# A decoder layer's feed-forward stage: Relu, squares and low part over two hidden units at a time

## The chip, the cores and the metric

The kernel runs on one core of a Trainium2 chip. The metric is the device time of one execution in microseconds (us), lower is better. The core has five engines that work in parallel, each from its own queue in order: PE (TensorE, matmuls), DVE (VectorE), ACT (ScalarE), POOL (GpSimd) and SP (SyncE, which issues DMAs here). They wait for each other through semaphores.

## The reference

A decoder layer over 8 batches of 512 tokens with 256 features: linear attention, cross-attention with 16 heads, and a feed-forward part, each followed by a layer norm. Only the feed-forward part matters here:

```python
def _bitlinear(x, w_latent):
    scale = jnp.clip(jnp.mean(jnp.abs(w_latent), axis=1, keepdims=True), 1e-05, None)
    tern = jnp.clip(jnp.round(w_latent / scale), -1.0, 1.0)
    return x @ (tern * scale).T          # in effect

h = _bitlinear(x, w_fc) + gate * (x @ v.T @ fast_b.T @ u.T)    # 256 -> 1024
r = jnp.maximum(h, 0.0)
y = _bitlinear(r * r, w_proj)                                  # 1024 -> 256
x = _layernorm(x + y)
```

## The kernel before

Activations lie with the features on the 128 partitions and a batch's 512 tokens along the columns. The three parts of the layer run one after the other; `ffn_phase` is the last. A batch is two tiles of 512 columns (features 0 to 127 and 128 to 255). The hidden layer of 1024 is eight tiles of 128 x 512, called units here, i = 0 to 7.

Full precision comes from splitting: a value is rounded to the type fp32r ("hi") and the rest is kept as a second fp32r tile ("lo"), and a product is summed from hi x hi, hi x lo and lo x hi. So a unit's hidden matmul is six PE instructions (`split_matmul`, L47 to L49). For each unit then
- ACT takes Relu from the unit's PSUM bank into the tile relu (`r`, L1280), and squares it with rounding into `h_hi` (L1284);
- POOL squares `r` in full precision into the tile relu2 (`rr`, L1242);
- DVE subtracts `h_hi` from `rr` and writes the low part `h_lo` (L1373, `hidden_lo`);
- PE projects with the ternary weights, `h_hi` and `h_lo` in turn (L1484, L1485).

`r` and `rr` hold four units in a ring (RH = 4). The units' PSUM banks are 0, 1, 2 and 7; bank 3 holds the statistics of the third norm (STAT3), bank 4 those of the second (STAT2), banks 5 and 6 the projection's output.

Two layer norms are woven between the units, written out by hand in each engine's queue. While batch b is in its units, the second norm of batch b+1 is made (names with a 2: mean by PE at L1455, `deviate2` on DVE, square on ACT at L1254, `sum_squares2` on DVE, variance by PE at L1459, root on ACT, `normalise2` on DVE, which ends with x_hi and x_lo, L1365 and L1367), and the third norm of batch b-1 (names with a 3: `residual` and `sum_y3` on DVE, mean at L1465, `deviate3`, `sum_squares3`, variance at L1469, `normalise3`, then the store). PE begins batch b+1 when x_lo of b+1 is there. DVE's queue in a batch is: residual, sum_y3, low parts 0 and 1, deviate2, low part 2, sum_squares2, low part 3, deviate3, low parts 4 and 5, sum_squares3, low parts 6 and 7, normalise2, the sum for the mean of b+2, normalise3. In the views a tile's name drops its number: `y_sum<-y` is sum_y3, `y_sum<-y_c` that of the second norm, `dev<-y,ps` is deviate3, `cx_lo` is x_lo, and both `r` and `rr` read "relu".

## Time and profile before

| what | us |
|---|---|
| median of 3 runs (lowest, highest) | 1464.99 (1464.03, 1467.11) |
| the profiled execution's own time | 1464.29 |
| its span, from first to last instruction | 1462.5 |
| granted clock of PE, mean over the span | 0.976 of full |

| engine | busy us | share |
|---|---|---|
| PE | 1364.8 | 93% |
| DVE | 961.9 | 66% |
| ACT | 807.1 | 55% |
| POOL | 618.5 | 42% |

The feed-forward stage is the last seventh of the span, from about 1235 us on; the rest belongs to the two attentions. A share over the whole span is a mean over stages with different limits. The views used are the table of stretches (busy time by engine in a window), the chain of waits (followed back from the last instruction to whatever released each step), the timeline of an engine, and the instruction groups. In a timeline, a row with x2 merges two instructions; what stands in brackets is the engine's idle time before it and who ended it. PE's matmuls overlap, so its busy time is not its time at peak.

### The profile page before, as it was taken

Reading aid. Unit: us, or ns where it says so; the run is one execution under the profiler, and the core shown is the slowest. Engines: PE = TensorE matmul, PEld = TensorE weight load, DVE = VectorE, ACT = ScalarE, POOL = GpSimd, SP = SyncE. Lnnn points to the kernel's source line nnn. Section 1 sums busy time; section 2 is a strip of 40 time slices with the busy share of each in tenths; the row PEclk is TensorE's granted clock in tenths of the full one; section 3 lists DMA queues with packets and bytes.
Section 4 is the critical chain, followed back from the end, with each engine's and each line's share of the span. In section 5 each row is a group of like instructions: output and inputs, shape, how many; then the busy total and the mean of one; then the engine's idle time right before and its main releaser. Section 6 shows DMA issues by size and latency. Waiting matters only on the chain. (4 is left out here: it accounts for less than half of the span.)

```text
span 1462.5 us, 20833 instructions
## 1 busy us (share of the span) xinstructions
PE 1364.8 (93%) x7068; PEld 881.2 (60%) x7068; DVE 961.9 (66%) x1819; ACT 807.1 (55%) x1062; POOL 618.5 (42%) x312
## 2 busy tenths in 40 slices
PE   6999759999999999999999999999999995799985
PEld 5777545557566565756656575665656553566663
DVE  5678636674765667466566746656674664699896
ACT  2334436664666556566655756665575654465653
POOL 3512004562544546255454725545472553343422
PEclk9999979999999999999999999999999998899997
DMA  5211120000100100010010000001001000011101
GB/s 183 85 58 58 58 90 1 1 1 8 54 0 1 59 0 0 15 44 0 0 59 0 0 25 34 0 0 59 0 0 41 4 1 24 19 44 43 44 15 43
DMA packets 25533, 42.84 MB, mean 29 GB/s; under 512 B 3440, under 2 KB 7936, under 8 KB 25488
## 3 DMA queue, kind: packets, MB, share of 16 engines
q1 hardware_dynamic: 24672, 39.10, 7.9%
q0 software_dynamic: 816, 3.15, 0.6%
q8 instruction: 27, 0.44, 0.1%
q14 instruction: 18, 0.15, 0.0%
HBM read 29.66 MB, written 12.58 MB: 29 GB/s over the span
## 5 line engine op out<-in xcount | busy, mean ns | idle before, releaser
L905 DVE CUSTOM_DVE_ANT_0 junk<-ps,mask 128x512 bf16<-128x512 f32 x512 | 319.9, 687 | 102.1 <-PE ps L1029 100.7
L727 POOL TENSOR_TENSOR acc<-prob 128x1024 f32<-128x1024 f32 x64 | 153.3, 2395 | 501.0 <-ACT prob L771 501.0
L771 ACT ACTIVATE prob<-ps,mcol 128x1024 f32<-128x1024 f32 x256 | 281.5, 1117 | 135.1 <-PE ps L1023 129.2
L730 POOL TENSOR_TENSOR acc<-acc,prob 128x1024 f32<-128x1024 f32 x128 | 304.1, 2376 | 11.5
L1044 PE MATMUL ps<-prob,v_b 128*64 128x512 f32 x1024 | 245.0, 599 | 0.0
L1044 PEld LDWEIGHTS ps<-prob,v_b 128*64 128x64 f32 x1024 | 69.2, 136 | 131.5 <-issue 107.6
L1242 POOL TENSOR_TENSOR relu<-relu 128x512 f32<-128x512 f32 x64 | 76.3, 1199 | 124.1 <-ACT relu L1280 121.7
L910 DVE TENSOR_TENSOR ps<-ps,recip 128x512 f32<-128x512 f32 x64 | 44.8, 699 | 116.6 <-ACT recip L786 116.5
L1021 PE MATMUL ps<-q_hi,k_hi 64*128 64x512 f32 x512 | 115.5, 445 | 3.1 <-ACT shift L798 1.6
L1029 PE MATMUL ps<-k_hi,q_hi 64*128 64x512 f32 x512 | 102.4, 393 | 2.7 <-DVE nmx L905 2.1
L1023 PE MATMUL ps<-shift,ones_r 64*128 64x512 f32 x512 | 102.0, 391 | 0.0
L1021 PE MATMUL ps<-q_hi,k_lo 64*128 64x512 f32 x512 | 101.9, 392 | 0.0
L1021 PE MATMUL ps<-q_lo,k_hi 64*128 64x512 f32 x512 | 101.7, 391 | 0.0
L923 DVE SCALAR_TENSOR_TENSOR att_lo<-ps,bv,att_hi 128x512 fp32r<-128x512 f32 x64 | 48.1, 751 | 54.3 <-ACT att_hi L794 54.3
L778 ACT ACTIVATE pvc<-ps 128x512 f32<-128x512 f32 x64 | 38.3, 599 | 81.7 <-PE ps L1044 81.7
L1021 PEld LDWEIGHTS ps<-q_hi,k_hi 64*128 64x128 f32 x512 | 48.3, 184 | 55.0 <-ACT prob L771 25.0
L784 ACT ACTIVATE recip<-ps 128x512 f32<-128x512 f32 x64 | 38.2, 598 | 77.1 <-PE ps L1052 77.1
L933 DVE SCALAR_TENSOR_TENSOR q_lo<-ps,bq,q_hi 128x512 fp32r<-128x512 f32 x64 | 48.1, 751 | 42.4 <-ACT q_hi L806 42.4
L1373 DVE TENSOR_TENSOR h_lo<-relu,h_hi 128x512 fp32r<-128x512 f32 x64 | 65.0, 1047 | 15.1 <-POOL relu L1242 15.1
L1052 PE MATMUL ps<-acc,ones_w 128*64 128x512 f32 x256 | 69.2, 618 | 5.0 <-DVE att_lo L923 2.5
L47 PE MATMUL ps<-cx_hi,wfc_hi 128*128 128x512 f32 x128 | 60.4, 472 | 9.4 <-DVE cx_lo L1367 9.4
L1280 ACT ACTIVATE relu<-ps 128x512 f32<-128x512 f32 x64 | 37.9, 592 | 52.8 <-PE ps L49 51.3
(204 smaller groups left out, 2896.8 us busy)
## 6 DMA issues: line engine op xcount, KB each, us to landing
x_in<-in_xT SPq DMA_DIRECT2D x8, 512.0 KB, 3.7
x_scratch<-x_a SPq DMA_DIRECT2D x8, 512.0 KB, 2.8
raw<-x_scratch SPq DMA_DIRECT2D x8, 512.0 KB, 5.0
raw<-in_cT SPq DMA_DIRECT2D x8, 512.0 KB, 5.8
x_res<-x_scratch SPq DMA_DIRECT2D x8, 512.0 KB, 4.5
y_scratch<-y SPq DMA_DIRECT2D x8, 512.0 KB, 3.2
y_c<-y_scratch SPq DMA_DIRECT2D x8, 512.0 KB, 3.7
outT<-x SPq DMA_DIRECT2D x8, 512.0 KB, 2.8
```

What stands on the lines that cost most here:

```text
L47: pe.matmul(out, lh, rh, start=(i == 0), stop=False)
L727: pool.tensor_tensor(total, prob[:, 0], prob[:, 1], ALU.add).then_inc(acc_out, 1)
L730: pool.tensor_tensor(total, total, prob[:, kt], ALU.add).then_inc(acc_out, 1)
L771: act.activation(prob[:, i].rearrange("p h t -> p (h t)"), SCORE[i % 2].rearrange("p h t -> p (h t)"), ACT.Exp, scale=SCALE, bias=mcol[:, ...
L905: dve.tensor_tensor_reduce(junk[:, t % 2, h], SMAX[t % 2][:, h], mask[:], -1.0, -LOWEST, ALU.add, ALU.min, nmx[:, t, h * DH:h * DH + 1]).t ...
L1021: pe.matmul(banks[:, h], l[OWN[h], par, cols], r[OWN[h], par], start=(n == 0), stop=False)
L1023: mm = pe.matmul(banks[:, h], ones_r[OWN[h], :], shift[OWN[h], :], start=False, stop=True)
L1029: mm = pe.matmul(SMAX[t % 2][:, h], q_hi[OWN[h], par, toks], k_hi[OWN[h], par], start=True, stop=True)
L1044: mm = pe.matmul(PV[OWN[h], :], v[:, kt, cols], prob[:, kt, h, :], start=(kt == 0), stop=(kt == NT - 1))
L1052: mm = pe.matmul(DEN[OWN[h], :], c["ones_w"][:, 0:DH], acc[:, par, h, :], start=True, stop=True)
L1242: pool.tensor_tensor(rr[:, n, :], r[:, n, :], r[:, n, :], ALU.mult).then_inc(rr_out, 1)
L1373: dve.tensor_tensor(h_lo[:, i, :], rr[:, i % RH, :], f32(h_hi[:, i, :]), ALU.subtract).then_inc(lo_out, 1)
```

## The change

The units are handled in pairs. A pair's two hidden tiles lie in neighbouring PSUM banks, (0, 1) or (2, 3), so STAT3 moves from bank 3 to bank 7. Relu, its square on ACT, POOL's square and DVE's low part each run once over 1024 columns, four times a batch instead of eight. The matmuls stay as they are: PE still computes and projects unit by unit, and waits for the Relu at the even units and for the low part of the pair that a unit belongs to. The ring of `r` and `rr` stays four units, that is two pairs. Semaphores count pairs, except `h_ps`. The places of the norms' instructions in the queues of ACT and DVE move with the pairs.

ACT's queue, start of batch 1: Relu (`relu<-ps`), its square (`h_hi<-relu`) and the square of deviate2's result (`sq<-dev`). Before:

```order
L1280 ACTIVATE relu<-ps 128x512 [waits c_rr_out,c_h_ps]
L1284 ACTIVATE h_hi<-relu 128x512 [waits c_p_ps,c_relu_out]
L1280 ACTIVATE relu<-ps 128x512 [waits c_rr_out,c_h_ps]
L1284 ACTIVATE h_hi<-relu 128x512 [waits c_relu_out]
L1280 ACTIVATE relu<-ps 128x512 [waits c_rr_out,c_h_ps]
L1284 ACTIVATE h_hi<-relu 128x512 [waits c_relu_out]
L1254 ACTIVATE sq<-dev 128x1024 [waits c_sq2_sum_out,c_dev2_out]
L1280 ACTIVATE relu<-ps 128x512 [waits c_rr_out,c_h_ps]
L1284 ACTIVATE h_hi<-relu 128x512 [waits c_relu_out]
```

Changed:

```order
L1282 ACTIVATE relu<-ps 128x1024 [waits c_rr_out,c_h_ps]
L1286 ACTIVATE h_hi<-relu 128x1024 [waits c_p_ps,c_relu_out]
L1255 ACTIVATE sq<-dev 128x1024 [waits c_sq2_sum_out,c_dev2_out]
L1282 ACTIVATE relu<-ps 128x1024 [waits c_rr_out,c_h_ps]
L1286 ACTIVATE h_hi<-relu 128x1024 [waits c_relu_out]
```

Three units stood ahead of `sq<-dev`, now one pair does.

DVE's queue, from sum_y3 to the last low part in the batch after the loop, the same in each batch but the first and the last. Before:

```order
L1318 TENSOR_TENSOR y_sum<-y 128x512 [waits c_mean3_ps,c_y3_out]
L1373 TENSOR_TENSOR h_lo<-relu,h_hi 128x512 [waits c_rr_out,c_hi_out] x2
L1343 TENSOR_TENSOR dev<-y_c,ps 128x1024 [waits c_x2_out,c_mean2_ps]
L1373 TENSOR_TENSOR h_lo<-relu,h_hi 128x512 [waits c_rr_out,c_hi_out]
L1318 TENSOR_TENSOR sq_sum<-sq 128x512 [waits c_var2_ps,c_sq2_out]
L1373 TENSOR_TENSOR h_lo<-relu,h_hi 128x512 [waits c_rr_out,c_hi_out]
L1387 TENSOR_TENSOR dev<-y,ps 128x1024 [waits c_x3_out,c_mean3_ps]
L1373 TENSOR_TENSOR h_lo<-relu,h_hi 128x512 [waits c_rr_out,c_hi_out] x2
L1335 TENSOR_TENSOR sq<-dev 128x1024 [waits c_dev3_out]
L1318 TENSOR_TENSOR sq_sum<-sq 128x512 [waits c_var3_ps,c_sq3_out]
L1373 TENSOR_TENSOR h_lo<-relu,h_hi 128x512 [waits c_rr_out,c_hi_out] x2
```

Changed:

```order
L1317 TENSOR_TENSOR y_sum<-y 128x512 [waits c_mean3_ps,c_y3_out]
L1373 TENSOR_TENSOR h_lo<-relu,h_hi 128x1024 [waits c_rr_out,c_hi_out]
L1342 TENSOR_TENSOR dev<-y_c,ps 128x1024 [waits c_x2_out,c_mean2_ps]
L1317 TENSOR_TENSOR sq_sum<-sq 128x512 [waits c_var2_ps,c_sq2_out]
L1373 TENSOR_TENSOR h_lo<-relu,h_hi 128x1024 [waits c_rr_out,c_hi_out]
L1388 TENSOR_TENSOR dev<-y,ps 128x1024 [waits c_x3_out,c_mean3_ps]
L1373 TENSOR_TENSOR h_lo<-relu,h_hi 128x1024 [waits c_rr_out,c_hi_out]
L1334 TENSOR_TENSOR sq<-dev 128x1024 [waits c_dev3_out]
L1317 TENSOR_TENSOR sq_sum<-sq 128x512 [waits c_var3_ps,c_sq3_out]
L1373 TENSOR_TENSOR h_lo<-relu,h_hi 128x1024 [waits c_rr_out,c_hi_out]
```

`sq_sum<-sq`, which waits for ACT's square, now follows `dev<-y_c,ps` at once, without a low part between; the other norm instructions keep their neighbours, in pairs.

The diff:

```diff
--- before.py
+++ after.py
@@ -1200,8 +1200,9 @@
     x_split, h_ps, relu_out, hi_out, rr_out, lo_out, p_ps, y3_out = sems(
         "x_split", "h_ps", "relu_out", "hi_out", "rr_out", "lo_out", "p_ps", "y3_out")
 
-    HIDDEN = [ps[:, i, :] for i in (0, 1, 2, 7)]
-    STAT3, STAT2 = ps[:, 3, :], ps[:, 4, :]
+    HP, RP = HK // 2, RH // 2
+    HIDDEN = [ps[:, 2 * i:2 * i + 2, :] for i in range(RP)]
+    STAT3, STAT2 = ps[:, 7, :], ps[:, 4, :]
     OUT = ps[:, 5:7, :]
 
     def both(tile):
@@ -1234,11 +1235,11 @@
             pool.tensor_copy(tern[:], c["tern"][:]).then_inc(tern_out, 1)
 
             def batch(b, first):
-                for i in range(HK):
-                    pool.wait_ge(relu_out, HK * b + i + 1)
-                    if not (first and i < RH):
-                        pool.wait_ge(lo_out, HK * b + i - RH + 1)
-                    n = i % RH
+                for j in range(HP):
+                    pool.wait_ge(relu_out, HP * b + j + 1)
+                    if not (first and j < RP):
+                        pool.wait_ge(lo_out, HP * b + j - RP + 1)
+                    n = slice(j % RP * 2, j % RP * 2 + 2)
                     pool.tensor_tensor(rr[:, n, :], r[:, n, :], r[:, n, :], ALU.mult).then_inc(rr_out, 1)
 
             batch(0, True)
@@ -1272,26 +1273,24 @@
             def norm3_root(b, first):
                 norm_root(STAT3, (est3, inv3), (var3_ps, est3_out, rs3_out), b, first)
 
-            def hidden(b, i, first):
-                n = HK * b + i
-                act.wait_ge(h_ps, n + 1)
-                if not (first and i < RH):
-                    act.wait_ge(rr_out, n - RH + 1)
-                act.activation(r[:, i % RH, :], HIDDEN[i % RH], ACT.Relu).then_inc(relu_out, 1)
+            def hidden(b, j, first):
+                n = HP * b + j
+                act.wait_ge(h_ps, 2 * n + 2)
+                if not (first and j < RP):
+                    act.wait_ge(rr_out, n - RP + 1)
+                two = slice(j % RP * 2, j % RP * 2 + 2)
+                act.activation(r[:, two, :], HIDDEN[j % RP], ACT.Relu).then_inc(relu_out, 1)
                 act.wait_ge(relu_out, n + 1)
-                if i == 0 and not first:
+                if j == 0 and not first:
                     act.wait_ge(p_ps, 2 * b)
-                act.activation(h_hi[:, i, :], r[:, i % RH, :], ACT.Square).then_inc(hi_out, 1)
+                act.activation(h_hi[:, 2 * j:2 * j + 2, :], r[:, two, :], ACT.Square).then_inc(hi_out, 1)
 
             def batch(b, first, second, last):
-                for i in (0, 1, 2):
-                    hidden(b, i, first)
+                hidden(b, 0, first)
                 if not last:
                     norm_square(dev2, sq2, dev2_out, sq2_out, sq2_sum_out, b + 1, False)
-                for i in (3, 4):
-                    hidden(b, i, first)
-                for i in (5, 6, 7):
-                    hidden(b, i, first)
+                for j in (1, 2, 3):
+                    hidden(b, j, first)
                 if not last:
                     norm2_root(b + 1, False)
                 if not first:
@@ -1366,11 +1365,13 @@
                 dve.wait_ge(x_split, 2 * b + 1)
                 dve.tensor_tensor(x_lo[:, par], x2[:, par], f32(x_hi[:, par]), ALU.subtract).then_inc(x_split, 1)
 
-            def hidden_lo(b, i):
-                n = HK * b + i
+            def hidden_lo(b, j):
+                n = HP * b + j
                 dve.wait_ge(hi_out, n + 1)
                 dve.wait_ge(rr_out, n + 1)
-                dve.tensor_tensor(h_lo[:, i, :], rr[:, i % RH, :], f32(h_hi[:, i, :]), ALU.subtract).then_inc(lo_out, 1)
+                two, at = slice(2 * j, 2 * j + 2), j % RP * 2
+                dve.tensor_tensor(h_lo[:, two, :], rr[:, at:at + 2, :], f32(h_hi[:, two, :]),
+                                  ALU.subtract).then_inc(lo_out, 1)
 
             def residual(b, par, first):
                 for m in range(DK):
@@ -1393,28 +1394,23 @@
                 dve.scalar_tensor_tensor(out=x3[:], in0=dev3[:], scalar=-0.5, in1=both(rs3), op0=ALU.mult,
                                          op1=ALU.mult).then_inc(x3_out, 1)
 
-            STAT2_T, STAT3_T = ps[:, 4, :], ps[:, 3, :]
+            STAT2_T, STAT3_T = ps[:, 4, :], ps[:, 7, :]
 
             def batch(b, par, first, second, last, next_last=False):
                 if not first:
                     residual(b - 1, 1 - par, second)
                     sum_y3(b - 1, second)
                 hidden_lo(b, 0)
-                hidden_lo(b, 1)
                 if not last:
                     deviate2(b + 1, False)
+                    sum_squares2(b + 1, False)
+                hidden_lo(b, 1)
+                if not first:
+                    deviate3(b - 1, second)
                 hidden_lo(b, 2)
-                if not last:
-                    sum_squares2(b + 1, False)
+                if not first:
+                    sum_squares3(b - 1, second)
                 hidden_lo(b, 3)
-                if not first:
-                    deviate3(b - 1, second)
-                for i in (4, 5):
-                    hidden_lo(b, i)
-                if not first:
-                    sum_squares3(b - 1, second)
-                for i in (6, 7):
-                    hidden_lo(b, i)
                 if not last:
                     normalise2(b + 1, 1 - par, False)
                 if not (last or next_last):
@@ -1471,15 +1467,15 @@
             def hidden(b, par, i, first):
                 if i == 0:
                     pe.wait_ge(x_split, 2 * b + 2)
-                if not (first and i < RH):
-                    pe.wait_ge(relu_out, HK * b + i - RH + 1)
+                if i % 2 == 0 and not (first and i < RH):
+                    pe.wait_ge(relu_out, HP * b + i // 2 - RP + 1)
                 cols = slice(i * P, (i + 1) * P)
-                split_matmul(pe, HIDDEN[i % RH], [(w_hi[:, k, cols], w_lo[:, k, cols], x_hi[:, par, k],
+                split_matmul(pe, HIDDEN[i // 2 % RP][:, i % 2], [(w_hi[:, k, cols], w_lo[:, k, cols], x_hi[:, par, k],
                                                    x_lo[:, par, k]) for k in range(DK)]).then_inc(h_ps, 1)
 
             def project(b, m, tiles):
                 for k in tiles:
-                    pe.wait_ge(lo_out, HK * b + k + 1)
+                    pe.wait_ge(lo_out, HP * b + k // 2 + 1)
                     w = tern[:, k, m * P:(m + 1) * P]
                     pe.matmul(OUT[:, m], w, h_hi[:, k, :], start=(k == 0), stop=False)
                     mm = pe.matmul(OUT[:, m], w, h_lo[:, k, :], start=False, stop=(k == HK - 1))
```

## Rows read from the trace of the kernel before

**Rows 1.** The page's part 1: busy us, share of the span, instructions.

```profile
PE 1364.8 (93%) x7068; PEld 881.2 (60%) x7068; DVE 961.9 (66%) x1819; ACT 807.1 (55%) x1062; POOL 618.5 (42%) x312
```

**Rows 2.** Stretches: window, length, busy us per engine, granted clock, DMA share, GB/s.

```profile
1240.00:1251.00 11.00, 2.08 (x2) 0.50 (x2) 7.79 (x9) 3.01 (x4) 0.00 (x0) 0.50 0.15 48
1251.00:1256.00 5.00, 4.40 (x11) 3.52 (x12) 1.06 (x2) 1.23 (x2) 0.79 (x1) 0.52 0.00 0
1350.00:1375.00 25.00, 22.58 (x89) 16.03 (x88) 22.84 (x26) 14.03 (x24) 9.11 (x9) 1.00 0.13 42
```

**Rows 3.** Chain of waits, feed-forward stage: start us, us, what ran.

```profile
1251.60 0.76 PE ps L47
...
1274.48 0.50 PE ps L47
...
1297.72 0.49 PE ps L47
...
1322.01 0.49 PE ps L47
...
1347.23 0.49 PE ps L47
...
1372.48 0.49 PE ps L47
...
1422.66 0.50 PE ps L47
```

**Rows 4.** Timeline of DVE, batch 4: start, us, line, operation, shapes, idle before.

```profile
1351.79 1.09 DVE L1318 TENSOR_TENSOR y_sum<-y 128x512 f32<-128x512 f32 x1
1352.80 2.15 DVE L1373 TENSOR_TENSOR h_lo<-relu,h_hi 128x512 fp32r<-128x512 f32 x2
...
1357.30 0.69 DVE L1318 TENSOR_TENSOR sq_sum<-sq 128x512 f32<-128x512 f32 x1 [0.61 <-ACT sq L1254]
1358.99 1.57 DVE L1373 TENSOR_TENSOR h_lo<-relu,h_hi 128x512 fp32r<-128x512 f32 x1 [1.00 <-POOL relu L1242]
1360.48 1.21 DVE L1387 TENSOR_TENSOR dev<-y,ps 128x1024 f32<-128x1024 f32 x1
1361.61 2.84 DVE L1373 TENSOR_TENSOR h_lo<-relu,h_hi 128x512 fp32r<-128x512 f32 x2
...
1367.43 0.74 DVE L1349 SCALAR_TENSOR_TENSOR rs<-ps,eps,inv 128x512 f32<-128x512 f32 x1
```

**Rows 5.** Timeline of ACT, batch 0 (first row) and batch 4.

```profile
1256.57 0.60 ACT L1280 ACTIVATE relu<-ps 128x512 f32<-128x512 f32 x1 [0.77 <-PE ps L49]
...
1350.37 0.60 ACT L1280 ACTIVATE relu<-ps 128x512 f32<-128x512 f32 x1
...
1356.20 1.06 ACT L1254 ACTIVATE sq<-dev 128x1024 f32<-128x1024 f32 x1 [2.32 <-DVE dev L1343]
1357.17 0.57 ACT L1280 ACTIVATE relu<-ps 128x512 f32<-128x512 f32 x1
...
1361.95 0.60 ACT L1280 ACTIVATE relu<-ps 128x512 f32<-128x512 f32 x1
```

**Rows 6.** Timeline of POOL, batch 4.

```profile
1349.76 2.57 POOL L1242 TENSOR_TENSOR relu<-relu 128x512 f32<-128x512 f32 x2 [11.10 <-ACT relu L1280]
...
1357.82 4.64 POOL L1242 TENSOR_TENSOR relu<-relu 128x512 f32<-128x512 f32 x4 [3.41 <-ACT relu L1280]
```

**Rows 7.** Instructions on tile relu: count, ns min/median/max, first and last start, shape.

```profile
L1242 POOL TENSOR_TENSOR relu<-relu x64: 1036/1064/2017, 1255.2 to 1435.6; 128x512 f32<-128x512 f32 x64
L1373 DVE TENSOR_TENSOR h_lo<-relu,h_hi x64: 676/693/1576, 1256.4 to 1439.5; 128x512 fp32r<-128x512 f32 x64
```

**Rows 8.** Groups by shape, whole span: count, busy us, mean ns, idle before.

```profile
L738 POOL TENSOR_TENSOR bc_lo<-raw,bc_hi 128x1024 fp32r<-128x1024 f32 x7 | 16.8, 2403 | 18.4 <-ACT bc_hi L826 18.4
...
L1367 DVE TENSOR_TENSOR cx_lo<-x,cx_hi 128x1024 fp32r<-128x1024 f32 x8 | 9.8, 1225 | 0.3
...
L241 POOL TENSOR_TENSOR wk_lo<-raw,wk_hi 128x512 fp32r<-128x512 f32 x4 | 5.1, 1276 | 0.3
```

More of the change, by code:

```diff
@@ L1402, in batch @@
                 hidden_lo(b, 0)
-                hidden_lo(b, 1)
                 if not last:
                     deviate2(b + 1, False)
-                hidden_lo(b, 2)
-                if not last:
                     sum_squares2(b + 1, False)
-                hidden_lo(b, 3)
+                hidden_lo(b, 1)
                 if not first:
                     deviate3(b - 1, second)
-                for i in (4, 5):
-                    hidden_lo(b, i)
+                hidden_lo(b, 2)
                 if not first:
                     sum_squares3(b - 1, second)
-                for i in (6, 7):
-                    hidden_lo(b, i)
+                hidden_lo(b, 3)
                 if not last:
```

## The prediction

> **What bounds the kernel now.** The change touches the feed-forward stage alone, so the share of busy time over the whole span [rows 1] says nothing of it; it is read by stage. The table of stretches [rows 2] gives one stretch of that stage: of 25.00 us DVE (VectorE) is busy 22.84, PE (TensorE) 22.58, ACT (ScalarE) 14.03 and POOL (GpSimd) 9.11. Neither of the two full ones is saturated, so the chain of waits is read next [rows 3]. It shows the first matmul of batches 0 to 5 and 7. The distances are 22.88, 23.24, 24.29 and 25.22 us for batches 0 to 3, and (1422.66 - 1347.23) / 3 = 25.14 for batches 4 to 6. Each batch begins when DVE has written x_lo, so DVE's queue sets the period, with what it waits for.
>
> I take batch 4 and write all times from its first matmul, 1347.23 = 0. The timeline of DVE [rows 4] shows: y_sum at 4.56 for 1.09, two low parts at 5.57 for 2.15 together, sq_sum of the next batch's norm at 10.07 behind an idle 0.61 for ACT, then 1.00 idle for POOL's square, the low part of unit 3 from 11.76 to 13.33 (1.57), two more in 2.84, and rs of normalise2 at 20.20. From rs to the next batch's first matmul are 25.25 - 20.20 = 5.05 (the next batch starts at 1372.48 [rows 3]).
>
> The low parts are the odd ones. One of 512 columns takes 0.676 us at best, 1.576 at worst [rows 7]. The long ones overlap a POOL square. POOL's squares of units 3 to 6 stand at 10.59 in one run of 4.64 [rows 6], 1.16 each; the low part at 11.76 ends only 0.5 us after the square of unit 4 has ended. y_sum ends at 5.65, 0.55 after POOL's pair (2.53 + 2.57 = 5.10). The deviation at 13.25 reads PSUM and one SBUF tile, lies under the same POOL squares and takes 1.21. So here DVE instructions with two SBUF inputs and POOL's squares take turns, and one that comes late waits for the other's whole instruction. In the Trainium skill, "SBUF — State Buffer", section "Who interferes with whom", such a DVE instruction and a GpSimd instruction that reads SBUF exclude one another and the second to issue blocks until the first finishes. By that rule, the trace agrees (1.57 against 0.68), and a POOL instruction twice as long blocks twice as long: it speaks against this change, and the schedule below would be the same with or without it.
>
> **Prices.** Relu of 1024 columns: ACT's square of 1024 took 1.06 and lets the next start 0.97 later (8.97 and 9.94 in [rows 5]); Relu and square of 512 cost about the same (0.60, 0.63), so 1.05. Low part of 1024: the same subtraction in x_lo, 1.225 [rows 8], with the next 1.15 later. POOL's square of 1024 has no row. Two of 512 are 2 x 1.04 = 2.08 [rows 7]. The fixed part: its subtraction takes 1.276 at 512 and 2.403 at 1024 [rows 8], a slope of 1.127 and a fixed 0.149 or so. Less that, 2.08 - 0.14 = 1.94, which I take, since it uses the same operation's own row; the upper bound is 2.40, the other operation's row at that size; below 1.94 there is no row, and I allow 1.8. In the Trainium skill, "GPSIMD Engine Reference", section "3.1 Elementwise — side-by-side cycle accounting", GpSimd needs some 2.6 cycles an element at two inputs, an estimate of 2.2 us for 1024; this trace's 1.04 for 512 is a little under it, and the sum below would by the page be about 9 us more.
>
> **The change part by part, for one steady batch** (P0 to P3 are the pairs of units):
> - *Relu of P0.* It waits for unit 1, whose Relu begins at 3.14 now [rows 5]: 3.14 to 4.19. POOL squares P0 from 4.27 to 6.21 (before, unit 0 was begun at 2.53).
> - *y_sum.* DVE comes to it at 4.56 as now, but POOL holds the ports till 6.21: it ends 0.55 later, at 6.76 against 5.65. mean3 on PE waits for it, 0.3 to 0.5 later than now; PE has room for that, since it waits for sq_sum at var2.
> - *Low part of P0*, 6.70 to 7.85. deviate2 starts there, 0.2 later than now, because the two single low parts also lost time to POOL. ACT's square of the deviation follows as now, 1.32 later: 9.17 (now 8.97).
> - *The queue on ACT.* Relu of P1 stands behind that square. It starts at 10.14 and ends at 11.19, and POOL's square of P1 runs 11.27 to 13.21. Before, unit 2 passed ahead of the deviation, and POOL began unit 3 at 10.59. So after this point now come three pairs, six units, where five units came, and they start 0.7 later.
> - *The shared stretch.* POOL's P2 and DVE's low part of P1 are ready together at 13.3. Whoever goes first, their work is in a row: with POOL first, P2 13.3 to 15.3, low part of P1 to 16.4, P3 16.5 to 18.4 (it also waits for that low part, since only two pairs of the relu2 tile exist), low part of P2 to 19.6, sq3 1.24 and sq3's sum 0.6 to 21.4, low part of P3 to 22.5. With DVE first, P2 14.8 to 16.8 and P3 to 18.8, and the low part of P2 lands within 0.4 of the same point. The Relu of P3 is no limit: unit 7's Relu stands at 14.72 now [rows 5].
> - *The end.* rs at 22.4 against 20.20: +2.2 us a batch. The check by counting: 0.7 of later start, one more square on the path (1.16), one more low part (0.64), less some 0.3 for fixed parts, is 2.2. The rest of DVE's queue is untouched: 22.4 + 5.05 = 27.4. PE has 20 matmuls left after the last low part; at 22.58 / 89 = 0.25 each [rows 2] they need 5.1, about the 5.05 of DVE: no new bound, but no slack either.
> - *What it saves:* ACT has 8 fewer instructions a batch, 8 x (0.61 - 0.5) or 0.9 us; ACT is 14.03 of 25 busy, so this is worth nothing beyond what the sizes above hold. Swapping STAT3 to bank 7, and the waits of PE on pairs, cost nothing: the Relu of P0 is long done when unit 4 starts, and unit 6 waits for the Relu of P1 (11.3) where var2 holds PE to about 11.7 anyway. SP's queue keeps its place; both its transfers stay off the chain.
>
> **Sum.** Batches 3 to 6: 27.4 less 25.22 and three times 25.14, 2.2 + 3 x 2.26 = +9.0. Batch 2 (24.29): +3.1. Batch 1 has no older normalise3 ahead of its y_sum, so that comes before POOL's P0, 0.4 sooner: 27.0 against 23.24, +3.7. Batch 0: the stretch from 1251 to 1256 runs at a granted clock of 0.52, after one in which PE was busy 2.08 of 11 us [rows 2], that is at the 1.2 GHz level, and the second Relu stands at 1256.57 - 1251.60 = 4.97 instead of 3.14 [rows 3, 5]. That puts the pair 1.83 later, y_sum is absent (-0.4), and so are sq3 and its sum (-1.85): 22.0 + 5 = 26.9 against 22.88, +4.0. Batch 7: taken as a steady one, +2.2. Together 9.0 + 3.1 + 3.7 + 4.0 + 2.2 = 22.0. The profiled execution took 1464.29 (span 1462.5 and 1.8 around it): 1486.3. The median of the runs is 0.7 above it: **1487.0**.
>
> **The rivals.**
> - *POOL at the upper price.* Four squares of the 8 batches on the path, 32 x (2.40 - 1.94) = +14.7: 1501. At 1.8 it is -4.5: 1482. At plain doubling, 2.08: 1491. For it speaks that spans on POOL are rough; against it that the square reads one tile twice and is cheaper at 512 (1.04 against 1.28).
> - *Faster: fewer encounters.* Half as many POOL and DVE instructions meet half as often. If DVE no longer waited at all, the low parts would fall from 5.57..13.33's 0.68 to 1.57 each to four of 1.23; with eight at a mean of about 1.05 [rows 4] that is 8.4 - 4.9 = 3.5 less on DVE, and PE's own 22.6 busy of 25 would then set the period, some 1.6 below 25.2: 8 x 1.6 = 13 less, 1452. It decides if POOL's squares fall into DVE's PSUM-reading or idle time. Against it: after the late Relu of P1 three POOL squares and three low parts have only one deviation (1.2) to hide under.
> - *No difference.* The pairs' delay is caught by slack: DVE's 0.61 and 1.00 idle before sq_sum and unit 3, and PE's. It would need the chain to hold 2 us of slack behind unit 3; DVE has no idle row there. 1465.
> - *The clock.* PE now waits longer in the second half of a batch (for the low parts of P1 and P2, over 2 us at once). If the grant fell to 1.2 GHz there, the last 20 matmuls would cost twice the fast pace of some 0.2: 8 x 4 = 32 more, 1519. Against it: the grant stays at 1.00 through 1350 to 1375 with several waits per batch [rows 2].
>
> **How the numbers follow.** The forecast with POOL between 1.8 and 2.1: 1480 to 1493, chance 0.68. POOL dearer, up to 1502: 0.15. Faster by encounters: 0.07. No difference: 0.06. Clock: 0.04. Range 1478 to 1502 holds the first two and leaves out the rest. Between the executions of before lie 0.2%, which is about what can be told from no change. Faster by over 0.2%: 0.07, within: 0.06, slower: 0.87.
>
> **What would show it.** Right: first matmuls of successive batches 27 to 28 us apart; y_sum of 1.9 to 2.3 us; low parts of 1024 over 2 us in places; POOL's square of 1024 near 1.94; ACT idle for deviate2 between P0 and P1 as before; PE waiting at projection tiles 2 and 4. Wrong: a period of 25 or less, low parts all near 1.2, a POOL square outside 1.8 to 2.4, or a granted clock under 1.00 inside the stage.

## The result, and the profile after

The changed kernel takes 1487.49 us, the median of 4 runs (1485.00 to 1493.32), against 1465.64 for the kernel before in 4 runs. The ratio is 1.0156, 95% interval 1.0134 to 1.0178: slower by 22 us. The profiled execution is the slowest of the four, 1493.32 with a span of 1491.5; its feed-forward stage also begins 4.5 us later than in the profile of before (1256.15 against 1251.60 for the first hidden matmul [rows 3]), which lies ahead of all that was changed: in after_again, the same kernel run again, it begins at 1254.33, in the other runs between 1251.34 and 1254.77. So stages are compared below, each batch from its own first matmul.

From the page of the changed kernel, answering [rows 1]: part 1 and the groups of POOL's square and DVE's low part.

```profile
PE 1382.4 (93%) x7068; PEld 891.3 (60%) x7068; DVE 946.3 (63%) x1787; ACT 796.0 (53%) x998; POOL 611.5 (41%) x280
...
L1243 POOL TENSOR_TENSOR relu<-relu 128x1024 f32<-128x1024 f32 x32 | 68.7, 2154 | 155.9 <-ACT relu L1282 155.1
...
L1373 DVE TENSOR_TENSOR h_lo<-relu,h_hi 128x1024 fp32r<-128x1024 f32 x32 | 50.3, 1574 | 51.4 <-POOL relu L1243 51.4
```

DVE, ACT and POOL are each less busy than before (DVE 946.3 against 961.9), and the kernel is slower: what was gained in busy time is not on the path. A low part of 1024 takes 1.574 us on the average, while the same form takes 1.225 undisturbed [rows 8].

Stretches of batches 2 to 4 of the changed kernel (columns as in [rows 2]); each ends where the next batch's first matmul starts.

```profile
1310.54:1338.02 27.48, 23.99 (x90) 17.00 (x88) 20.59 (x21) 12.97 (x15) 8.61 (x4) 0.94 0.12 39
1338.02:1367.02 29.00, 25.48 (x90) 18.06 (x88) 22.24 (x24) 12.96 (x15) 8.62 (x4) 0.88 0.11 37
1367.02:1395.24 28.22, 25.39 (x89) 17.98 (x88) 20.24 (x21) 12.97 (x15) 8.61 (x4) 0.88 0.11 37
```

Their lengths are 27.48, 29.00 and 28.22 us where the kernel before has 24.29, 25.22 and 25.25, and the granted clock is 0.94, 0.88 and 0.88 where it was 1.00. All the batches, first matmul to first matmul:

| batch | 0 | 1 | 2 | 3 | 4 | 5 | 6 |
|---|---|---|---|---|---|---|---|
| before | 22.88 | 23.24 | 24.29 | 25.22 | 25.25 | 25.15 | 25.03 |
| changed | 26.82 | 27.56 | 27.48 | 29.00 | 28.22 | 27.70 | 27.57 |
| forecast | 26.9 | 27.0 | 27.4 | 27.4 | 27.4 | 27.4 | 27.4 |

Batch 4 begins at 1367.02. DVE (answers to [rows 4]), then ACT and POOL ([rows 5, 6]) in it:

```profile
1369.14 0.69 DVE L1317 TENSOR_TENSOR y_sum<-y 128x512 f32<-128x512 f32 x1
1373.19 1.22 DVE L1373 TENSOR_TENSOR h_lo<-relu,h_hi 128x1024 fp32r<-128x1024 f32 x1 [3.37 <-POOL relu L1243]
...
1379.71 1.23 DVE L1373 TENSOR_TENSOR h_lo<-relu,h_hi 128x1024 fp32r<-128x1024 f32 x1 [2.26 <-POOL relu L1243]
...
1382.79 2.83 DVE L1373 TENSOR_TENSOR h_lo<-relu,h_hi 128x1024 fp32r<-128x1024 f32 x1 [0.73 <-POOL relu L1243]
...
1388.53 0.75 DVE L1348 SCALAR_TENSOR_TENSOR rs<-ps,eps,inv 128x512 f32<-128x512 f32 x1
...
1392.21 1.23 DVE L1366 TENSOR_TENSOR cx_lo<-x,cx_hi 128x1024 fp32r<-128x1024 f32 x1
```

```profile
1370.01 1.02 ACT L1282 ACTIVATE relu<-ps 128x1024 f32<-128x1024 f32 x1 [7.27 <-PE ps L49]
...
1375.66 1.06 ACT L1255 ACTIVATE sq<-dev 128x1024 f32<-128x1024 f32 x1 [3.44 <-DVE dev L1342]
1376.63 1.01 ACT L1282 ACTIVATE relu<-ps 128x1024 f32<-128x1024 f32 x1
...
1371.20 1.89 POOL L1243 TENSOR_TENSOR relu<-relu 128x1024 f32<-128x1024 f32 x1 [15.65 <-ACT relu L1282]
1377.71 6.83 POOL L1243 TENSOR_TENSOR relu<-relu 128x1024 f32<-128x1024 f32 x3 [4.62 <-ACT relu L1282]
```

The picture of the forecast is there. ACT squares the deviation at 8.64 (1375.66 - 1367.02) and only then takes the Relu of P1, at 9.61; POOL has its last three squares in one run of 6.83 us from 10.69. The low part of P2 (1382.79) is ready, meets POOL's square of P3 and takes 2.83 us instead of 1.23. The last low part ends at 21.6 and rs starts at 21.51, where rs stood at 20.20 before. What is not as forecast: y_sum takes 0.69 and was never held up, DVE having come to it 0.9 us ahead of the Relu of P0; and x_lo ends at 1393.44, 1.8 us ahead of the next batch. PE is the one that comes late. PE in the last third of the batch: the first projection behind its wait, then the two passes of var3 and the projections behind them:

```profile
1385.68 0.79 PE L1480 MATMUL ps<-h_hi,tern_r 128*128 128x512 f32 x1 [2.46 <-DVE h_lo L1373]
...
1387.55 2.06 PE L1465 MATMUL ps<-sq_sum,mean_w 128*128 128x512 f32 x2
1388.67 1.37 PE L1480 MATMUL ps<-h_hi,tern_r 128*128 128x512 f32 x1
1389.84 0.63 PE L1481 MATMUL ps<-h_lo,tern_r 128*128 128x512 f32 x1
1390.26 0.63 PE L1480 MATMUL ps<-h_hi,tern_r 128*128 128x512 f32 x1
```

PE waits 2.46 us for the low part of P2, and the matmuls behind the wait start 0.43 us apart (1389.84, 1390.26), twice the 0.23 of the rest; var3 takes 2.06 for its two passes where it took 1.12 in the kernel before. This is the lower of the clock's two levels, 1.2 GHz. It came after PE's longest wait, in each batch from 1 to 7, with 1 to 9 slow projections. In batch 0 PE waits as long, 2.47 us, and the grant stays up, so the length of the wait alone does not decide it.

### The profile page after: what moved, and what is told of

Read it like the earlier page. It is cut to its first block and busy times, and to the rows that moved or that the text cites. A ratio compares the mean times of both kernels' runs of the same rounds, so it can differ in the third digit from the quotient of the medians.

```text
span 1491.5 us, 20545 instructions
## 1 busy us (share of the span) xinstructions
PE 1382.4 (93%) x7068; PEld 891.3 (60%) x7068; DVE 946.3 (63%) x1787; ACT 796.0 (53%) x998; POOL 611.5 (41%) x280
## 5 line engine op out<-in xcount | busy, mean ns | idle before, releaser
L730 POOL TENSOR_TENSOR acc<-acc,prob 128x1024 f32<-128x1024 f32 x128 | 303.9, 2374 | 11.5
L1243 POOL TENSOR_TENSOR relu<-relu 128x1024 f32<-128x1024 f32 x32 | 68.7, 2154 | 155.9 <-ACT relu L1282 155.1
L1373 DVE TENSOR_TENSOR h_lo<-relu,h_hi 128x1024 fp32r<-128x1024 f32 x32 | 50.3, 1574 | 51.4 <-POOL relu L1243 51.4
L1480 PE MATMUL ps<-h_hi,tern_r 128*128 128x512 f32 x128 | 60.6, 474 | 17.3 <-DVE h_lo L1373 17.3
L1282 ACT ACTIVATE relu<-ps 128x1024 f32<-128x1024 f32 x32 | 32.6, 1019 | 64.4 <-PE ps L49 64.4
```

Source lines behind the costliest of these rows:

```text
L730: pool.tensor_tensor(total, total, prob[:, kt], ALU.add).then_inc(acc_out, 1)
L1243: pool.tensor_tensor(rr[:, n, :], r[:, n, :], r[:, n, :], ALU.mult).then_inc(rr_out, 1)
L1373: dve.tensor_tensor(h_lo[:, two, :], rr[:, at:at + 2, :], f32(h_hi[:, two, :]), ALU.subtract).then_inc(lo_out, 1)
L1480: pe.matmul(OUT[:, m], w, h_hi[:, k, :], start=(k == 0), stop=False)
```

## The experiments

Ratios are to the kernel before, with runs on the same chip. The diffs are against the kernel named in the expectation.

### e1_fill: keep PE at work in its longest wait

```diff
-                project(b, 0, range(0, 6))
+                project(b, 0, range(0, 4))
+                if not first:
+                    pe.wait_ge(dev3_out, b)
+                    for _ in range(9):
+                        pe.matmul(STAT3, tern[:, 0, 0:P], h_hi[:, 0, :], start=True, stop=True)
+                project(b, 0, (4, 5))
```

> The changed kernel with nine spare matmuls (ternary weights by h_hi into bank 7, overwritten later) on PE ahead of the wait for the low part of P2, where PE now idles 2.5 us. Nothing else moves. Theory A, the clock costs: in the changed kernel's trace the grant falls to 0.5 in each batch after PE's wait, and the projections behind it run at 0.43 us; batches start 27.5 to 29.0 us apart, though the last low part ends at 21.6. With the wait filled the grant stays 1.00, the period is 26.6 to 27.0, and the run is 5 to 9 us under the changed kernel's 1487.5: 1479 to 1483. Theory B, PE is only late because the low parts are: no change within 2 us, 1486 to 1490, and the slow matmuls vanish without gain.

1484.92 us, ratio 1.0131 (1.0114 to 1.0148). Stretches of batches 3 and 4, and DVE's y_sum and rs in batch 4, which begins at 1362.62:

```profile
1335.57:1362.62 27.05, 25.47 (x97) 17.74 (x98) 22.30 (x22) 12.98 (x15) 8.62 (x4) 1.00 0.11 39
1362.62:1389.66 27.04, 25.47 (x98) 17.76 (x98) 22.29 (x22) 12.98 (x15) 8.62 (x4) 1.00 0.11 39
```

```profile
1367.18 2.19 DVE L1317 TENSOR_TENSOR y_sum<-y 128x512 f32<-128x512 f32 x1
...
1384.62 0.74 DVE L1348 SCALAR_TENSOR_TENSOR rs<-ps,eps,inv 128x512 f32<-128x512 f32 x1
```

The grant is 1.00 and the period 27.05 and 27.04. PE is in time again, so y_sum now comes after POOL's square of P0 has begun and takes 2.19 us, as the prediction had it; the last low part ends at 22.1 instead of 21.6. So part of what the clock costs is hidden by a wait that it spares. In batch 0, which had no filling, eight projections were slow and the batch took 28.4. The gain over the changed kernel, 2.6 us, is under the 5 to 9 us expected, but the two were not run side by side: hence the next two runs.

### e9_fill_all and after_again: the clock's price on one chip

```diff
+                if first:
+                    pe.wait_ge(lo_out, 2)
+                    for _ in range(6):
+                        pe.matmul(STAT3, tern[:, 0, 0:P], h_hi[:, 0, :], start=True, stop=True)
```

> The changed kernel with spare matmuls ahead of PE's wait for the low part of P2 in every batch, batch 0 too (six there, nine elsewhere). In e1_fill batch 0 was left as it is and took 28.4 us with eight slow projections. Theory A: the grant holds at 1.00 from the second unit of batch 0 to the last batch, batch 0 takes 26.0 to 26.8 us, batches 2 to 6 27.0 as in e1_fill, and the run is 1 to 2 us under e1_fill: 1482 to 1484.5. Theory B, the fall of the clock does not hang on that idle stretch: slow projections stay in batch 0.

> The changed kernel unaltered, on the same chip as these runs, for the differences of e9_fill_all: 1485 to 1490, with the grant falling to 0.5 in most batches and a number of slow projections that need not be the same per batch.

1484.02 (1.0118, 1.0101 to 1.0135) and 1489.70 (1.0151, 1.0134 to 1.0168). One stretch each from the start of batch 1 to the start of batch 7, first e9_fill_all, then after_again:

```profile
1278.97:1440.18 161.21, 151.91 (x584) 106.60 (x583) 129.81 (x124) 77.88 (x90) 51.70 (x24) 1.00 0.10 33
```

```profile
1281.95:1449.30 167.35, 147.17 (x529) 104.35 (x528) 123.48 (x124) 77.80 (x90) 51.71 (x24) 0.92 0.09 32
```

161.21 us at a grant of 1.00 against 167.35 at 0.92: six batches cost 6.1 us more, 1.0 each, and batch 0 another 0.9 (26.69 against 27.61). With the medians, 5.7 us of the 22.5 between the changed kernel and the one before on this chip are the clock. The other 17 are there with the grant held up. No projection is slow in batch 0 of e9_fill_all, so theory A holds.

### e2_interleave: fewer projections behind the last low part

```diff
-                project(b, 0, range(0, 6))
+                project(b, 0, range(0, 4))
+                project(b, 1, range(0, 4))
+                project(b, 0, (4, 5))
+                project(b, 1, (4, 5))
                 if not first:
                     var3(b - 1)
                 project(b, 0, (6, 7))
-                project(b, 1, range(HK))
+                project(b, 1, (6, 7))
```

> The changed kernel with the projection's order on PE changed: tiles 0 to 3 of both output halves, then 4 and 5 of both, then var3, then 6 and 7 of both. So 8 matmuls instead of 20 follow the last low part, and 8 of the 12 moved ones fill the wait for P2. Theory A, the end of a batch is now PE's (it starts the next one 1.1 to 2.6 us after x_lo is there): the next batch starts 0.1 us after x_lo again, y_sum is then blocked by POOL's square of P0 (over 1.2 us), the period is 26.6 to 27.0 and the run 1477 to 1482. Theory B, DVE's low parts set everything: 1486 to 1490.

1491.52, ratio 1.0187 (1.0167 to 1.0207), slower than the changed kernel and outside both expectations. PE at the end of batch 4:

```profile
1386.40 0.39 PE L1481 MATMUL ps<-h_lo,tern_r 128*128 128x512 f32 x1
1389.60 0.49 PE L47 MATMUL ps<-cx_hi,wfc_hi 128*128 128x512 f32 x1 [2.81 <-DVE cx_lo L1366]
...
1390.43 0.63 PE L47 MATMUL ps<-cx_hi,wfc_hi 128*128 128x512 f32 x1
1390.86 0.63 PE L48 MATMUL ps<-cx_lo,wfc_hi 128*128 128x512 f32 x1
```

The next batch does start right behind x_lo, as theory A had it. But PE is now through 2.81 us before that, the clock falls in or right behind this wait, and the slow ones are the hidden matmuls: 6 to 10 of them in four batches, with the Relu of P0 at 4.6 to 5.6 us instead of 3.1. The wait was moved, not removed, and moved ahead of work on which all the batch hangs. Batch 3, where the hidden matmuls ran fast behind a wait of 2.79 us, took 27.03.

### e3_order512: the order alone

```diff
-                for i in (0, 1, 2):
+                for i in (0, 1):
                     hidden(b, i, first)
                 if not last:
                     norm_square(dev2, sq2, dev2_out, sq2_out, sq2_sum_out, b + 1, False)
-                for i in (3, 4):
+                for i in (2, 3, 4):
                     hidden(b, i, first)
...
-                hidden_lo(b, 2)
                 if not last:
                     sum_squares2(b + 1, False)
+                hidden_lo(b, 2)
```

> The kernel before, all instructions at 512 columns as they were, with the changed kernel's order alone: ACT squares the deviation after unit 1 instead of unit 2, DVE's deviate2 and sum_squares2 stand together ahead of the low part of unit 2. Theory A, the order costs (unit 2's Relu, POOL square and low part move behind the deviation, onto the stretch that sets the end): one square and one low part more there, 1.2 to 1.8 us a batch in seven batches, 1474 to 1479. Theory B, the width costs (a 1024-column instruction holds the shared ports twice as long): 1464 to 1467.

1470.30, ratio 1.0038 (1.0023 to 1.0052): slower by 5.3 us, where theory A said 9 to 14 and theory B nothing. In batch 4 (from 1354.46) POOL's last squares are one run of six, and DVE's low parts of units 2 and 3 stand in their shadow:

```profile
1364.26 7.45 POOL L1242 TENSOR_TENSOR relu<-relu 128x512 f32<-128x512 f32 x6 [4.70 <-ACT relu L1280]
...
1360.03 1.28 DVE L1373 TENSOR_TENSOR h_lo<-relu,h_hi 128x512 fp32r<-128x512 f32 x2
...
1365.40 2.96 DVE L1373 TENSOR_TENSOR h_lo<-relu,h_hi 128x512 fp32r<-128x512 f32 x2 [1.06 <-POOL relu L1242]
...
1375.24 0.74 DVE L1349 SCALAR_TENSOR_TENSOR rs<-ps,eps,inv 128x512 f32<-128x512 f32 x1
```

rs stands at 20.78 against 20.20: in a steady batch the order costs 0.6 of DVE's schedule, not 1.8. Two rows of POOL in batch 4 of the kernel before, to set beside these and [rows 6]:

```profile
1353.37 1.04 POOL L1242 TENSOR_TENSOR relu<-relu 128x512 f32<-128x512 f32 x1 [1.04 <-ACT relu L1280]
...
1362.62 1.28 POOL L1242 TENSOR_TENSOR relu<-relu 128x512 f32<-128x512 f32 x1 [0.17 <-ACT relu L1280]
```

There the square of unit 2 (1353.37) met the low part of unit 1, and the two low parts took 2.15; here they take 1.28, deviate2 and the square behind it come earlier, and POOL's last run starts at 9.80 instead of 10.59. From there six squares take 7.45 where five took 6.08 (10.59 to 16.67). One square more, 1.37, less the start 0.79 sooner, is the 0.6. In batches 0 and 1, where the clock stayed up too, the order costs more, 1.2 and 1.4 (24.08 and 24.66 against 22.88 and 23.24). Some of the total is the clock again, which falls in three batches of this run. In batch 4 PE waits three times, and var3 behind the third takes 2.07:

```profile
1370.86 0.50 PE L1483 MATMUL ps<-h_hi,tern_r 128*128 128x512 f32 x1 [0.72 <-DVE h_lo L1373]
...
1372.31 0.50 PE L1483 MATMUL ps<-h_hi,tern_r 128*128 128x512 f32 x1 [0.72 <-DVE h_lo L1373]
...
1374.17 2.07 PE L1468 MATMUL ps<-sq_sum,mean_w 128*128 128x512 f32 x2 [1.12 <-DVE sq_sum L1318]
```

In batches 5 and 6 PE waits 0.71 to 0.72 and 1.13 us; the grant falls in batch 5 and stays up in batch 6.

### e6_pooldve512: whose width it is

```diff
-                for j in range(HP):
-                    pool.wait_ge(relu_out, HP * b + j + 1)
+                for i in range(HK):
+                    pool.wait_ge(relu_out, HP * b + i // 2 + 1)
...
-                dve.tensor_tensor(h_lo[:, two, :], rr[:, at:at + 2, :], f32(h_hi[:, two, :]),
-                                  ALU.subtract).then_inc(lo_out, 1)
+                for i in (2 * j, 2 * j + 1):
+                    dve.wait_ge(rr_out, HK * b + i + 1)
+                    dve.tensor_tensor(h_lo[:, i, :], rr[:, i % RH, :], f32(h_hi[:, i, :]),
+                                      ALU.subtract).then_inc(lo_out, 1)
```

> The changed kernel with POOL's squares and DVE's low parts back at 512 columns, unit by unit; Relu and rounded squares on ACT stay at 1024, and the order stays. Tells whose width matters. Theory A, it is the pair's late Relu and the same work in a row: little changes, 1481 to 1489. Theory B, it is the long hold of the shared ports: most of the 16 us between this order at 512 columns (1470.3) and the changed kernel comes back, 1470 to 1475.

1490.10, ratio 1.0165 (1.0148 to 1.0182), 1.1 over the range of theory A: nothing comes back, and theory B falls. With the clock up, batches 2 and 3 take 27.28 and 27.29, against 27.05 in e1_fill. In batch 4 (from 1363.22):

```profile
1374.53 7.37 POOL L1243 TENSOR_TENSOR relu<-relu 128x512 f32<-128x512 f32 x6 [4.52 <-ACT relu L1282]
...
1385.44 0.74 DVE L1348 SCALAR_TENSOR_TENSOR rs<-ps,eps,inv 128x512 f32<-128x512 f32 x1
```

The six squares take 7.37 us one by one against 6.83 as three pairs, so POOL's and DVE's wider instructions help a little: rs at 22.22 here, 22.00 in e1_fill. Against e3_order512, which has the same order and differs only in ACT's width (with the waits that go by ACT's pairs), POOL's run starts at 11.31 instead of 9.80 and rs stands at 22.22 instead of 20.78. That is the pair on ACT: its Relu waits for two units (3.1 against 1.8 us), deviate2 comes 1.1 later for it, and POOL then waits for a Relu of 1.01 instead of 0.58.

### e4_p1first and e8_order4_512: the other order, at both widths

```diff
                 hidden(b, 0, first)
+                hidden(b, 1, first)
                 if not last:
                     norm_square(dev2, sq2, dev2_out, sq2_out, sq2_sum_out, b + 1, False)
-                for j in (1, 2, 3):
+                for j in (2, 3):
                     hidden(b, j, first)
```

> The changed kernel with ACT's order changed alone: Relu and square of P1 ahead of the square of the deviation; 1024 columns stay. Theory A, the order costs: Relu of P1 then starts at about 6.6 instead of 9.6 in a batch, POOL squares P1 from 7.7, the last square ends near 18.1 and the last low part near 19.4 instead of 21.6; period 24.5 to 25.3, 1456 to 1466. Theory B, the width costs: the period stays above 26.5, 1480 or more.

> The kernel before at 512 columns with the order of run e4_p1first: ACT squares the deviation after unit 3, DVE has deviate2 and sum_squares2 after the low part of unit 1. With e3, e4, before and changed it completes orders by widths. Theory A, order and width act together (the pair drags unit 3 behind the deviation): here only the order differs from before, one square and one low part less after it, period 24.0 to 25.0, 1456 to 1464, and e4 minus this is the width's own price, 2 to 8 us. Theory B, the width has no price of its own: the same as e4, 1466 to 1468.

1466.82 (1.0017, 1.0006 to 1.0027) and 1467.08 (1.0003, 0.9994 to 1.0013). One swap on ACT takes 20 of the 22 us back. Of the 20, 5 to 6 are the clock, which no longer falls in batches 0 to 6: against e9_fill_all, where it does not fall either, the ratio goes from 1.0118 to 1.0017, 15 us. Theory A had the period (24.66) and was 0.8 us too low at the top of its range. In batch 4 of e4_p1first (from 1350.55) ACT's Relu of P1 and DVE's y_sum, the sum of squares and rs:

```profile
1357.21 1.02 ACT L1282 ACTIVATE relu<-ps 128x1024 f32<-128x1024 f32 x1 [1.34 <-PE ps L49]
...
1355.11 2.18 DVE L1318 TENSOR_TENSOR y_sum<-y 128x512 f32<-128x512 f32 x1
...
1366.85 2.27 DVE L1318 TENSOR_TENSOR sq_sum<-sq 128x512 f32<-128x512 f32 x1
...
1370.18 0.74 DVE L1349 SCALAR_TENSOR_TENSOR rs<-ps,eps,inv 128x512 f32<-128x512 f32 x1
```

The Relu of P1 starts at 6.66 instead of 9.61, rs at 19.63. Two DVE sums of 0.69 are held for 2.18 and 2.27 by POOL's longer squares; still the steady period is 24.66, 0.6 under the kernel before. What it wins there goes in batch 0, 25.54 us against 22.88, where the pair waits for two units at the slow clock (its Relu starts at 5.12, unit 0's in the kernel before at 2.93), and in batch 1, 23.97 against 23.24. With e8_order4_512 at 25.07 in steady state and 23.30 in batch 0, both end level. For e8_order4_512 theory A is refuted: its order is no faster than that of the kernel before, and the time is the one that theory B gave. Medians of all six cells (each with its own chip's ratio above):

| ACT squares the deviation | 512 columns | Relu and rounded square at 1024 |
|---|---|---|
| after unit 1 | 1470.3 (e3) | 1487.5 (changed), 1490.1 (e6) |
| after unit 2 | 1465.6 (before) | not possible in pairs |
| after unit 3 | 1467.1 (e8) | 1466.8 (e4) |

Width costs about nothing in one order and 17 us in the other. Of the 17, 5 to 6 are the clock: by the ratios of e9_fill_all and e3 it is 12. The move of STAT3 to bank 7 and PE's waits on pairs are in e4 too, so they have no visible price either.

### e5_rr_on_act and e7_before_rr_act: no turns with POOL

The full-precision square moves from POOL to ACT, in the changed kernel and in the kernel before. The edit in the first:

```diff
                 act.activation(h_hi[:, 2 * j:2 * j + 2, :], r[:, two, :], ACT.Square).then_inc(hi_out, 1)
+                if not (first and j < RP):
+                    act.wait_ge(lo_out, n - RP + 1)
+                act.activation(rr[:, two, :], r[:, two, :], ACT.Square).then_inc(rr_out, 1)
```

> The changed kernel with the full-precision square of each pair on ACT (1.06 us, right after the rounded one) and POOL idle in this stage. Order and widths stay. Theory A, turns between POOL and DVE are on the path: no DVE instruction of two SBUF inputs is ever long again (all low parts 1.22, sums 0.69), ACT carries 4 us more a batch, the last low part ends near 20.0 instead of 21.6, the period is 25.0 to 25.8, 1464 to 1472. Theory B, ACT's queue alone sets the path and POOL costs nothing: ACT's longer queue makes it later, 1490 to 1496.

> The kernel before (512 columns, its own order) with the full-precision square on ACT and POOL idle in this stage. Theory A, turns with POOL cost DVE some 3 us a batch in the kernel before too: low parts all 0.68, DVE busy about 20 a batch, the last low part ends near 18, the period falls to 22.6 to 23.4, set by PE; 1446 to 1454. Theory B, they are hidden: 1463 to 1470, or later since ACT has 4.4 us more.

1475.69 (1.0065, 1.0048 to 1.0082) and 1461.42 (0.9965, 0.9954 to 0.9976). All low parts of e5_rr_on_act (count, ns min/median/max):

```profile
L1369 DVE TENSOR_TENSOR h_lo<-relu,h_hi x32: 1217/1226/1228, 1259.7 to 1448.5; 128x1024 fp32r<-128x1024 f32 x32
```

1217 to 1228 ns, where the changed kernel has up to 2832: the long ones were POOL's doing. The period falls to 25.72 and 12 us come back, though ACT has 4 us more in a batch. The clock has a part in the 12, since it stays up in batches 1 to 6 here; against e9_fill_all, where it does too, the period falls from 27.04 to 25.72 and 8 us come back. The expected 25.0 to 25.8 was right, the total 4 us over it, since batch 0 took 28.1 with six slow projections. In the kernel before the same step makes it faster, by less than theory A said and more than theory B (the period is 24.09, the last low part ends at 17.9): DVE then waits for ACT's root:

```profile
1366.90 0.69 DVE L1368 TENSOR_TENSOR h_lo<-relu,h_hi 128x512 fp32r<-128x512 f32 x1 [0.18 <-ACT relu L1279]
1368.73 0.75 DVE L1344 SCALAR_TENSOR_TENSOR rs<-ps,eps,inv 128x512 f32<-128x512 f32 x1 [1.14 <-ACT inv L1259]
```

### e10_split: a version faster than both

```diff
+    ON_ACT = {0: 1, 1: 2, 2: 3, 3: 4, 5: 5, 7: 6}
+    ON_POOL = {4: 1, 6: 2}
...
-                for i in range(HK):
+                for i in (4, 6):
...
+                if i in ON_ACT:
+                    if not (first and i < RH):
+                        act.wait_ge(lo_out, n - RH + 1)
+                    act.activation(rr[:, i % RH, :], r[:, i % RH, :], ACT.Square).then_inc(rr_out, 1)
```

> The kernel before at 512 columns with the full-precision squares of units 4 and 6 on POOL and those of the other six on ACT (a version meant to beat both kernels). In e7_before_rr_act ACT is the one that ends the batch: it works without a gap from the square of the deviation to the root, and DVE waits 1.14 us for the root. Theory A: ACT's queue gets 1.1 us shorter, at most two low parts meet POOL, the period falls from 24.1 to 23.0 to 23.5, the run to 1454 to 1459. Theory B, the turns with POOL take back what ACT gains: 1461 to 1465.

1454.37 us, ratio 0.9915 (0.9898 to 0.9931). Batch 4:

```profile
1344.72:1367.78 23.06, 22.28 (x88) 16.37 (x89) 20.29 (x26) 17.03 (x29) 3.16 (x2) 1.00 0.14 46
```

```profile
L1386 DVE TENSOR_TENSOR h_lo<-relu,h_hi x64: 678/686/695, 1256.9 to 1428.9; 128x512 fp32r<-128x512 f32 x64
```

The period is 23.06 with PE busy 22.28 of it, ACT 17.03 and no low part over 0.695, as theory A had it.

## Why the prediction was right, and where not

The sign holds, and so does the mechanism on ACT, POOL and DVE. That the time came so near (1487.0 against 1487.5) is luck: by the medians of e9_fill_all and after_again the schedule without the clock costs 16.8 us where 22.0 were forecast, and the fall of the clock, for which the sum had nothing, costs 5.7.

- **Prices.** POOL's square of 1024 took 1.894 us at the median (1.94 taken, from the same operation at 512 less another's fixed part), Relu 1.025 (1.05), the low part 1.22 undisturbed (1.225). The upper price for POOL, 2.40, was far off.
- **The queue on ACT.** As said: Relu of P1 behind the square of the deviation, three POOL squares in a row. e4_p1first removes exactly this and 20 us with it, 5 to 6 of them the clock.
- **How much later DVE is.** Forecast: rs at 22.4. With the clock up, in e1_fill, it is 22.00, so +1.8 and not +2.2. Up to POOL's square of P1 each step of e1_fill stands within 0.1 of the schedule (y_sum ends at 6.75, forecast 6.76; POOL's run of three starts at 11.18, forecast 11.27). The 0.4 was lost in the shared stretch: POOL's last square ends at 18.0, where 18.4 was forecast, or 18.8 with DVE first. The check by counting came to the same 2.2 with terms that do not stand: it took a full square and a low part for the unit that moved behind the deviation. The runs split it otherwise: the order 0.6 (20.20 to 20.78, e3), the pairs on ACT 1.4 (to 22.22, e6), POOL and DVE in pairs -0.2 (to 22.00, e1).
- **y_sum held by POOL.** Wrong for the changed kernel (0.69), right for e1_fill and e9_fill_all (2.2). It hung on PE being in time.
- **"No new bound, but no slack either" for PE, and the clock at 0.04.** These were the steps that failed. PE's wait for P2 was foreseen, "over 2 us at once", but that the grant stays up was argued from a stretch in which PE's longest wait was 1.1 us. The grant did fall, in seven of eight batches, which the prediction itself had named as a sign of being wrong, and from batch 1 on PE starts the next one 1.1 to 2.6 us behind x_lo. The size was wrong the other way: 32 us were priced, for 20 slow matmuls in each batch; there were 1 to 9 in seven of them, and e9_fill_all against after_again puts it at 5.7 us. PE did not wait for the low part of P1 at all.
- **The sum.** First matmul of batch 0 to the end of DVE, 232.2 against 207.7 us in the two profiles, +24.5 where 22.0 was forecast: batches 0 to 2 +11.5 (10.8), batches 3 to 6 +11.9 (9.0), batch 7 +1.2 (2.2). In e9_fill_all, with the clock up, the same stretch is 225.7, +18.0: batches 0 to 2 +9.7, batches 3 to 6 +7.2, batch 7 +1.1. Batches 3 to 6 are where the schedule was most too long.
- **The rivals.** "Fewer encounters": the encounters are fewer, but each is longer (2.83 against 1.57), and three in a row remain. "No difference": no slack showed. Who goes first when both are ready shows in the trace. In batch 4 DVE's low part of P1 starts at 1379.71 and is not held (1.23); the square of P2 starts 0.01 us later, is held and takes 2.98. At the next meeting POOL is first, and the low part of P2 takes 2.83.

```profile
1379.72 2.98 POOL relu L1243
1382.79 2.84 DVE h_lo L1373
```


## What to carry to other kernels

Merging small instructions into wider ones changes the order as well as the size: ask what now stands behind the instruction that a long chain waits for. Here the width was free once the second pair went ahead of that instruction. A wait on PE that grows past what the old profile shows has to be priced with some of the matmuls behind it at half clock, and a step that only moves the wait moves that price too, perhaps to a worse place.

## What the runs showed of the hardware

- The grant fell to the 1.2 GHz level behind single PE waits of 2.46 us (changed) and 2.81 us (e2), and also in e3 behind three waits of 0.72, 0.72 and 1.12 us close together. Equal waits did not always do it: it stayed up behind 2.47 us in batch 0 of the changed kernel, and in e6_pooldve512 waits of 1.14, 0.71 and 1.13 us left it up in batches 2 and 3, while it fell in batch 4 with waits of 1.15 and 0.71. It stayed up through a batch with one wait of 1.76 us in e7. How many projections ran slow changed from batch to batch in an otherwise equal schedule: 9, 8, 3, 2 and 1 in batches 3 to 7.
- Spare matmuls in the wait kept it up: 1.00 against 0.92 over the six batches, some 160 us, at a gain of 1.0 us a batch.
- DVE instructions with two SBUF inputs and POOL's squares exclude each other for the whole instruction at both sizes: with POOL out of the stage all 32 low parts took 1.217 to 1.228 us (e5) and all 64 of 512 columns at most 0.695 (e7), with it up to 2.832 and 1.576. ACT squaring the same tiles in POOL's place held up none of them.
- A square on POOL costs 1.04 us at 512 columns and 1.89 at 1024: by these two an estimate of a fixed 0.18 us and 1.68 ns a column, less than a subtraction of two tiles into fp32r (1.28 and 2.40).
